# Experts that gather their rows and add weighted results to x1 by accumulating DMAs, in place of a slot scatter

## The reference

```
x1 = layernorm(x + attention(x))                    # (2, 2048, 256)
logits = layernorm(x1, rn_g, rn_b) @ router_w.T + router_b
top_w, top_idx = top_k(logits, 2);  top_w = softmax(top_w)
out = 0
for e in range(8):
    h = layernorm(x1, ln_g[e], ln_b[e])             # same mean and variance, own scale and shift
    h = gelu(h @ w1[e] + b1[e]);  h = h @ w2[e] + b2[e]
    out += combine[..., e] * h                      # combine is top_w where e was chosen, else 0
result = layernorm(x1 + out)
```

## Time and profile before

| what | value |
|---|---|
| median of 3 runs | 3681.25 us (3676.75 to 3688.88) |
| the profiled execution's own time | 3678.63 us |
| its span in the profile | 3677.0 us |
| busy in the span: PE / VectorE / ACT / POOL | 3195.2 / 2888.1 / 2443.3 / 291.8 us |
| mean granted clock of PE | 0.926 of full |

### The profile page before, as it was taken

The page is one execution under the profiler, slowest core; times in us unless marked ns, Lnnn a source line. Parts: engine busy times, 40 slices in busy tenths (PEclk is TensorE's granted clock), DMA queues, the critical chain, the costliest instruction groups (busy, mean ns, idle before and its releaser), DMA issues. The chain is left out here.

```text
span 3677.0 us, 85882 instructions
## 1 busy us (share of the span) xinstructions
PE 3195.2 (87%) x29585; PEld 1513.9 (41%) x29586; DVE 2888.1 (79%) x3223; ACT 2443.3 (66%) x4499; POOL 291.8 (8%) x506
## 2 busy tenths in 40 slices
PE   7849999999999999999999999999844549999970
PEld 3413333333333333333333333333334448999960
DVE  2269999999999999999999999999957503334335
ACT  3309998998999999999899999899801001111110
POOL 0020000000000000000000000000023260000016
PEclk9959999999999999999999999999966659999985
DMA  4520101101011010110110101101064531111114
GB/s 114 125 45 21 28 8 39 28 8 29 21 28 26 24 25 20 30 28 8 39 28 8 29 21 28 26 24 25 16 243 156 202 125 35 37 36 37 36 57 148
DMA packets 127607, 184.40 MB, mean 50 GB/s; under 512 B 23272, under 2 KB 97560, under 8 KB 124412
## 3 DMA queue, kind: packets, MB, share of 16 engines
q1 hardware_dynamic: 119388, 151.03, 15.7%
q0 software_dynamic: 7296, 26.22, 2.1%
q10 hardware_dynamic: 544, 2.10, 0.2%
HBM read 105.36 MB, written 73.93 MB: 49 GB/s over the span
## 5 line engine op out<-in xcount | busy, mean ns | idle before, releaser
L558 DVE TENSOR_REDUCE half_max<-scores 128x2 f32<-128x1024 f32 x2096 | 2387.3, 1212 | 78.8 <-PE scores L461 75.2
L532 ACT ACTIVATE probs<-bank 128x512 f32<-128x512 f32 x4104 | 2227.1, 595 | 211.3 <-PE bank L480 144.4
L512 PE MATMUL bank<-probs,V 128*32 128x256 f32 x16384 | 1319.0, 394 | 68.9 <-ACT probs L532 39.2
L461 PE MATMUL scores<-K,Q 48*128 48x512 f16 x4192 | 832.6, 394 | 50.7 <-DVE half_max L558 24.7
L480 PE MATMUL bank<-Q,K 50*128 50x512 f16 x4104 | 796.0, 381 | 0.3 <-ACT probs L532 0.3
L461 PEld LDWEIGHTS scores<-K,Q 48*128 48x128 f16 x4192 | 201.4, 93 | 940.9 <-DVE half_max L558 739.6
L512 PEld LDWEIGHTS bank<-probs,V 128*32 128x32 f32 x16384 | 323.3, 108 | 628.5 <-issue 545.8
L480 PEld LDWEIGHTS bank<-Q,K 50*128 50x128 f16 x4104 | 375.9, 94 | 117.0 <-ACT probs L532 5.8
L1260 ACT ACTIVATE h<-u 128x1024 f32<-128x1024 f32 x71 | 75.0, 1057 | 420.6 <-DVE u L1287 420.6
L1229 PE MATMUL pre<-xgT,w 128*128 128x128 f32 x2272 | 267.4, 276 | 3.2 <-ACT xgT L1256 2.6
L1229 PEld LDWEIGHTS pre<-xgT,w 128*128 128x128 f32 x2272 | 266.8, 193 | 7.3 <-DVE w L1279 3.8
(11 more groups left out here) (151 smaller groups left out, 1143.0 us busy)
## 6 DMA issues: line engine op xcount, KB each, us to landing
heads<-attended SPq DMA_DIRECT2D x5, 4096.0 KB, 12.9
attended<-att SPq DMA_DIRECT2D x64, 256.0 KB, 2.5
W<-in_L_ffn_w_dram SPq DMA_DIRECT2D x14, 1024.0 KB, 11.6
Q<-q_parts SPq DMA_DIRECT2D x96, 128.0 KB, 5.2
K<-k_parts SPq DMA_DIRECT2D x96, 128.0 KB, 5.6
slot_rows<-zeros POOLq DMA_DIRECT2D x8, 1152.0 KB, 5.2
xg<-slot_rows SPq DMA_DIRECT2D x71, 128.0 KB, 2.0
slot_results<-y SPq DMA_DIRECT2D x71, 128.0 KB, 1.7
```

Of the source, the lines that this page charges most:

```text
L461: mm = nc.tensor.matmul(scores[:, b, h, :], Q[p][r, c, up, t * P:(t + 1) * P], K[p][r, up, kc * TC:(kc + 1) * TC], start=True, stop=True)
L512: mm = nc.tensor.matmul(banks[att_bank[s // KB]][32 * u:32 * u + 32, q], V[wp][:, wk, u // 2, :], probs[:, 4 * s % RING + u, q], start=(wk ...
L532: nc.scalar.activation(probs[:, i % RING, :], banks[tile_bank[i]][:], ACT.Exp, scale=SCALE).then_inc(exp_done, 1)
L558: nc.vector.tensor_reduce(half_max[lc % 2][:, :, up, t, kc], scores[:, b], AX.X, ALU.max).then_inc(max_done[b], 1)
```

## The change

Nothing is scattered into slots, and no result is stored by slot. The route stage turns its table round: for every slot of a tile it works out which token it holds. For each column t of 128 tokens and each choice r VectorE writes a one-hot row of the slot's place in its tile (`row_hot`, 128 columns) and one of its tile times the token's code (`tile_hot`, 72 columns), and a matmul of the two adds the code to the right cell of `coded`; 64 matmuls give the whole table. From it come, in `routes`, three indices for each slot: the row of `xh` to read, the row of `x1` to add to (an empty slot gets one of 128 spare rows behind the 4096), and the place of its weight in `combd`, a new table of token times expert in DRAM.

POOL then gathers the 128 rows of a tile and its 128 weights just before the tile is computed. `ln_g` and `ln_b` are no longer folded into `W1`: ACT applies them, in two instructions with pointers, as it copies the transposed rows. ACT also multiplies `y` by the weights (`ys`), and POOL adds `ys` to `x1` in DRAM with an indirect DMA that accumulates. A token appears in two tiles, so each of these DMAs waits until the one before has landed (`added`). The finish stage then only normalises `x1`. Its row order in DRAM is changed so that a partition's rows lie together. The zeros of `xgd` are no longer written; all 8 `w1` matrices and `b2s` are loaded in the route stage.

```diff
-    xgd = nc.dram_tensor("slot_rows", (NTL * TS, D), F32, kind="Internal").ap()
-    ygd = nc.dram_tensor("slot_results", (USED * TS, D), F32, kind="Internal").ap()
+    x1d = nc.dram_tensor("x1", (T + P, D), F32, kind="Internal").ap()
+    combd = nc.dram_tensor("expert_shares", (T * E, 1), F32, kind="Internal").ap()
...
-        stage_scatter(nc, locals())
...
+            for r in range(2):
+                chain.add(nc.vector.tensor_tensor(part_of[r][:], hot[r][:], over_e(share[r][:]), ALU.mult))
+            chain.wait()
+            nc.vector.tensor_tensor(comb[:], part_of[0][:], part_of[1][:], ALU.add).then_inc(comb_ready, 1)
...
+            for r in range(2):
+                for t in range(NT):
+                    nc.vector.tensor_scalar(row_hot[:, r, t, :], lane[:], place_f[0][:, r, t:t + 1], None, ALU.is_equal
+                                            ).then_inc(hot_ready, 1)
+                    nc.vector.tensor_scalar(tile_hot[:, r, t, :], lane[:, 0:NTL], place_f[1][:, r, t:t + 1],
+                                            token[:, t:t + 1], ALU.is_equal, ALU.mult).then_inc(hot_ready, 1)
+            step(nc.vector.tensor_scalar(owner[:], owner[:], float(E - 1), None, ALU.min))
+            dve.wait_ge(coded_ready, 1)
...
+            def gather(n, q):
+                nc.gpsimd.tensor_copy(cur[q][:], routes[:, bass.ds(n, 1), :].rearrange("p o f -> p (o f)")
+                                      ).then_inc(cur_ready, 1)
+                pool.wait_ge(cur_ready, n + 1)
+                pool.sem_inc(gate, 1)
+                nc.gpsimd.indirect_dma_start(xg[q][:], None, xhd,
+                                             bass.IndirectOffsetOnAxis(ap=cur[q][:, 0:1], axis=0)
+                                             ).then_inc(xg_loaded[q], 16)
+                nc.gpsimd.indirect_dma_start(part[q][:], None, combd,
+                                             bass.IndirectOffsetOnAxis(ap=cur[q][:, 2:3], axis=0)
+                                             ).then_inc(part_loaded[q], 16)
...
+            def step(n, it, q, left):
+                if not isinstance(n, int) or n > 0:
+                    pool.wait_ge(added, 16 * n)
+                if left >= FAR:
+                    if not isinstance(n, int) or n > 0:
+                        pool.wait_ge(turned, n)
+                    pool.wait_ge(ys_ready, n + 2)
+                    pool.sem_inc(gate, 1)
+                    gather(n + FAR, (q + FAR) % GB)
+                pool.wait_ge(ys_ready, n + 3)
+                pool.sem_inc(gate, 1)
+                nc.gpsimd.indirect_dma_start(x1d, bass.IndirectOffsetOnAxis(ap=cur[q][:, 1:2], axis=0),
+                                             ys[q % 2][:], None, compute_op=ALU.add).then_inc(added, 16)
...
-            def copy_rows(n, p):
+            def norm_rows(n, p):
+                e = owner(act, n)
                 act.wait_ge(turned, n + 1)
-                nc.scalar.copy(xgT[p][:], pxT[:, 0:D]).then_inc(xgT_ready, 1)
+                for k in range(KD):
+                    nc.scalar.activation(xgT[p][:, k * P:(k + 1) * P], pxT[:, k * P:(k + 1) * P], ACT.Identity,
+                                         scale=ln_cols[:, 0, bass.ds(e, 1), k], bias=ln_cols[:, 1, bass.ds(e, 1), k]
+                                         ).then_inc(xgT_ready, 1)
...
+            def weigh(n, it, q):
+                act.wait_ge(part_loaded[q], 16 * (it + 1))
+                act.wait_ge(y_ready, n + 3)
+                if not isinstance(n, int) or n > 1:
+                    act.wait_ge(added, 16 * (n - 1))
+                nc.scalar.activation(ys[q % 2][:], y[q % 2][:], ACT.Copy, scale=part[q][:, 0:1]).then_inc(ys_ready, 1)
...
+            for n in range(NC):
+                sp.dma_start(z[:, n], x1d[0:T].rearrange("(p n j) d -> n p j d", p=P, n=NC)[n]).then_inc(z_loaded[n], 16)
...
+            for n in range(NC):
+                moments(n)
+                if n > 0:
+                    normalise(n - 1)
+            normalise(NC - 1)
```

More of the change, by code:

```diff
@@ L304, in stage_attend @@
         att_stored = [sem(f"att_stored{i}") for i in range(2)]
[L305 to L309, removed]
+        gate_pool, gate_dve = sem("gate_pool"), sem("gate_dve")
         ROWS = [(h, i) for i in range(len(Q_PARTS)) for h in range(2)]
@@ L446, in _ @@
                     cut_maxima(it * RC + lc + 2)
[L447 to L450, removed]
         @block.tensor
@@ L1062, in _ @@
             for r in range(2):
-                step(nc.vector.tensor_tensor(took[r][:], hot[r][:], place[:], ALU.mult))
-                step(nc.vector.tensor_reduce(slot_f[r][:], took[r][:], AX.X, ALU.add))
-                nc.vector.tensor_copy(slot[r][:], slot_f[r][:]).then_inc(slots_ready, 1)
-def stage_scatter(nc, a):
-    xhd, xgd, slot, D, E, KD, NCH = (a[n] for n in ("xhd", "xgd", "slot", "D", "E", "KD", "NCH"))
-    EARLY = a["EARLY"]
-    w1, b2, W1, b1c, b2s, ln_cols, IC = (a[n] for n in ("w1", "b2", "W1", "b1c", "b2s", "ln_cols", "IC"))
+                chain.add(nc.vector.tensor_tensor(took[r][:], hot[r][:], place[:], ALU.mult))
@@ new lines, in _, with stage_experts @@
+            step(nc.vector.tensor_tensor(offset[:], above[:], below[:], ALU.add))
+            step(nc.vector.tensor_tensor(goal[0][:], code[:], offset[:], ALU.add))
+            chain.add(nc.vector.tensor_tensor(goal[1][:], goal[0][:], empty[:], ALU.add))
+            step(nc.vector.scalar_tensor_tensor(goal[2][:], goal[0][:], float(E), owner[:], ALU.mult, ALU.add))
+            for i in range(3):
+                nc.vector.tensor_copy(routes[:, :, i], goal[i][:])
+def stage_experts(nc, a):
+    xhd, x1d, combd, W1, W2, b1c, b2s, owner_i, routes, ln_cols = (
+        a[n] for n in ("xhd", "x1d", "combd", "W1", "W2", "b1c", "b2s", "owner_i", "routes", "ln_cols"))
+    KD, IC, D, E, I, USED, ident = (a[n] for n in ("KD", "IC", "D", "E", "I", "USED", "ident"))
+    GB = 4
+    FAR = GB - 1
@@ L1207, in _ @@
-            for n in range(2):
-                load(n, n)
-            for n in range(2):
-                sp.wait_ge(turned, n + 1)
-                load(n + 2, n)
-            run(sp, step)
-            for p in range(2):
-                sp.wait_ge(y_stored[p], 16 * ((USED + 1 - p) // 2) + 1)
+            for s in (y_ready, ys_ready):
+                sp.sem_inc(s, 2)
+            sp.wait_ge(added, 16 * USED)
+        @block.gpsimd
+        def _(pool):
+            def gather(n, q):
[22 more added lines that the diff above has]
+                                             ys[q % 2][:], None, compute_op=ALU.add).then_inc(added, 16)
+            for n in range(FAR):
+                gather(n, n)
+            run(pool, step)
```

368 lines of the change are left out of this document (144 added, 224 removed).

## The result

The changed kernel takes **3622.5 us**, median of 4 runs (3614.7 to 3626.0), against 3679.7 for the kernel before: a ratio of 0.985 [0.983, 0.986]. The forecast was 3532, with 3508 to 3612 as its range. So 57 us were gained where 149 were forecast, and the time lies 10 us above the range.

What follows compares the result with a forecast made beforehand. PE bounds the experts, GpSimd's issuing the scatter and finish: 3677.0 - 106.5 + 22.5 + 1.8 + 10.5 + 2.5 - 79.5 = 3528.3, plus 1.6 and 2.6 gives 3532.5 us; eight in ten, 3508 to 3612.

Steps and rivals of the forecast that it cites:

- Experts, each tile: Expert tiles: GpSimd's serial loop takes 7.4 us a cycle, 0.15 over PE's 7.25, times 70 = +10.5 us.
- the term that I feared most: Accumulating scatter's landing in GpSimd's loop: 1.65 us as plain, plus 0.7 for adding in DRAM, between 0 and 1.89.
- Scatter issue 0.98: GpSimd's loop in each expert tile: issuing the accumulating scatter takes 0.98 us.
- 0.2 for VectorE beside it: Expert tiles: VectorE's copy of `w1` lengthens GpSimd's scatter issue by 0.1 to 0.2 us; 0.2 charged per cycle.
- (1): Expert tiles: GpSimd's loop clearly bounds, an added row costing near the upper end; cycle 8.3, 3595 us, chance 0.18.
- (2): Expert tiles: VectorE's `w1` copy holds up GpSimd's issuing for the whole 1.23 us; cycle 8.4, 3605 us, chance 0.09.
- (3): Expert tiles: ScalarE makes PE wait 0.3 us per tile through dynamic operands and the owner's register load; 3543 us, chance 0.08.
- (4): Expert tiles: slower than before, rows of an accumulating scatter added one after another; cycle 18.3, 4295 us, chance 0.04.
- -106.5: Slot scatter stage goes: 64 scatters (81 us), the wait for the first `xh` load and the last W1 fold; -106.5 us.
- one-hot pairs: Route stage, VectorE: 64 pairs of `row_hot` (0.13) and `tile_hot` (0.15), 17.9 us, part of the route's +22.5 us.
- Start and end: Experts stage: start +1.8 us (5.1 in place of 3.3), end +2.5 us (5.1 in place of 2.6).
- Finish: Finish stage: eight 512 KB loads with moments and normalising, 36.4 us in place of 115.9, -79.5 us; bounds 33 and 46.

Runs made afterwards that it cites:

- experiment 1: Changed kernel with the addition left out of the scatter to `x1` (plain store, sums not the reference's): 3546.2 us.
- experiment 5: Changed kernel in which VectorE copies only one column of each `w1` matrix after the first two tiles: 3574.8 us.
- experiment 3: Changed kernel with eight gather buffers and the gathers for tile n+3 issued before the wait for the last accumulating DMA: 3538.6 us, 0.962 of before.
- experiment 8: Changed kernel with the zeros of `xgd` written again: 3619.7 us; also retraced unedited, the kernel before (3676.3 and 3677.8) and the changed one (3615.9).
- experiment 4: Changed kernel with eight gather buffers instead of four, GpSimd's queue order left as it is: 3609.0 us.
- experiment 7: Kernel that gathers before the wait (3538.6 us), with GpSimd writing the 32 `tile_hot` rows of the second choice: 3538.2 us.
- experiment 2: Changed kernel with VectorE's copy of `w1` written as a multiplication by 1.0: 3617.9 us.

## Why the prediction was wrong

The direction and the places were right; the forecast gain was 92 us too large (149 for 57). To compare the stages I take the third trace of before (span 3676.1) and the second of the changed kernel (3614.0), which entered the route stage within 1.4 us of each other. They are 62.1 apart where the forecast had 148.7:

```profile
2917.71 0.42 DVE L1019 TENSOR_REDUCE best<-lg 128x32 f32<-128x256 f32 x1
L1279 DVE COPY w<-W x71: 1216/1227/1228, 3036.1 to 3540.7; 128x2048 f32 x71
L1298 DVE TENSOR_TENSOR y<-py,b2s x71: 423/425/426, 3054.5 to 3557.6; 128x256 f32<-128x256 f32 x71
L1360 POOL MEMSET f_minus_half<- x1: 101/101/101, 3560.2 to 3560.2; 128x4 f32 x1
```

```profile
2919.11 0.42 DVE L1050 TENSOR_REDUCE best<-lg 128x32 f32<-128x256 f32 x1
L1290 DVE COPY w<-W x71: 1220/1227/1440, 2965.0 to 3551.9; 128x2048 f32 x71
L1310 DVE TENSOR_TENSOR y<-py,b2s x71: 423/425/426, 2987.9 to 3569.9; 128x256 f32<-128x256 f32 x71
L1349 POOL MEMSET f_minus_half<- x1: 102/102/102, 3581.5 to 3581.5; 128x4 f32 x1
```

| piece | before | after | measured | forecast |
|---|---|---|---|---|
| up to the route's first maximum | 2917.7 | 2919.1 | +1.4 | 0 |
| from there to the first copy of `w1` | 118.4 | 45.9 | -72.5 | -84.0 |
| to the first `y` (start) | 18.4 | 22.9 | +4.5 | +1.8 |
| 70 tiles | 503.1 | 582.0 | +78.9 | +10.5 |
| last `y` to the finish | 2.6 | 11.6 | +9.0 | +2.5 |
| finish | 115.9 | 32.5 | -83.4 | -79.5 |

**Experts, each tile: the step that failed**, 68 of the 87 us. The structure was right, all in series on POOL's queue. So was the term that I feared most: landing and the wait behind it came to 2.5 us where 1.65 + 0.7 + 0.3 = 2.65 stood. Two other terms were mis-sized. "Scatter issue 0.98" was taken from a plain scatter; with the addition it is 1.63 (experiment 1), +0.65. I had put the whole price of adding on the DMA engines and none on the engine that issues. "0.2 for VectorE beside it" is 0.68 (experiment 5), +0.48. 7.4 + 0.65 + 0.48 - 0.15 = 8.4, for 8.31 to 8.34 measured. PE's pace, 7.19 on average, was the floor, and the forecast cycle stood just above it; so nothing of this was absorbed and every bit counted 70 times.

**The 0.2** came from a row that I read for its length and not for where it ended. In the earlier trace rows the issue of 1.06 us ended at 2936.61. The first of the two multiplications beside it ended at about 2936.49 (an estimate: they take 0.75 us each, one behind the other from 2935.74), 0.12 before, just as beside the copies of `w1`. Alone the issue would have ended at 2936.51, so little was added; how much depends on where the two meet. The longest of the 64 took 1.27 in the same trace, and 1.44 in the third, where VectorE had begun just before. The "DVE blocks DMA" trap that the prediction weighed (the Trainium skill, page SBUF — State Buffer, section on the two sides of SBUF) says that GpSimd is locked out and cannot write descriptors until the copy ends. The trace agrees: no gather that began less than 0.5 us before a copy, or during it, ended before the copy did. What this costs depends on how much of the copy is still to come: 0.4 to 1.0 us for one issue, 0.68 per tile over the loop. The rule held, and by my reading of one row I had set it aside.

**The rivals.** (1) gave a cycle of 8.3 and that is what came, but from the issuing and not from the landing, which that rival blamed; its number was right by luck. (2) had the mechanism right. Its 1.23 was the upper end of the cost, and I had the accumulating DMA's issue fall on the copy, where it is one of the gathers that does. (3) did not come: ScalarE's two pieces took 0.79 where 0.5 was forecast, which the 0.51 to spare still covered, and in experiment 3 PE never waited. (4) did not come: 128 rows land in 2.5. No rival let two terms be wrong at once, and the range ended just above (2) alone; the two terms that were wrong together lie outside it.

**Route and scatter, +11.5.** -106.5 was true of one execution; the other two spent 7.4 us less there (experiment 8). I had read that the fold ended that stage, and not asked how often it does. The one-hot pairs took 0.37 us each and not 0.28 (the first pair, and the instruction behind the last one, in the first trace of the changed kernel):

```profile
2942.05 0.26 DVE L1111 TENSOR_SCALAR row_hot<-lane,place_f 128x128 f16<-128x128 f16 x1
2942.22 0.30 DVE L1113 TENSOR_SCALAR tile_hot<-lane,place_f,token 128x72 f16<-128x72 f16 x1
2965.74 0.23 DVE L1115 TENSOR_SCALAR owner<-owner 128x72 f32<-128x72 f32 x1
```

That is 23.7 for 17.9, within the bounds of 10 to 31; the route grew by 26.9 for 22.5. PE's matmuls were hidden and W1's loads covered, as said.

**Start and end.** In the table's trace the first product began 7.2 us after POOL's first index copy, where 5.1 were forecast. Of the 2.1 us more, 1.4 are one issue, the first gather's: it ran beside two copies of `w1` in a row (2965.01 to 2967.37), took 2.34 us in place of 0.98 and ended 0.14 us behind them. The clock hardly counts in this pair: PE's first two products took 5.6 and 3.8 us, and 5.3 and 3.8 before. In the first trace of the changed kernel they took 6.4 and 6.7, and the start was 3.6 us longer. There the granted clock was 0.50 all through the route stage, in which PE was busy for 17.9 of 47.7 us, rose after the first product had begun, and stood at 0.64 on average in the second window above: both products ran in part or wholly at the lower level, 1.2 GHz, and PE had stood still for 3.1 us between them. At the end:

```profile
3580.09 0.42 DVE L1310 TENSOR_TENSOR y<-py,b2s 128x256 f32<-128x256 f32 x1 [3.03 <-PE py L1241]
3582.98 1.56 POOL L1206 DMA_INDIRECT x<-ys,cur  x1 [2.98 <-DMA x<-ys,cur]
3591.72 0.10 POOL L1349 MEMSET f_minus_half<- 128x4 f32 x1 [7.18 <-POOLq L1137]
```

The last DMA waited for the one before (2.98), which I had not counted. With 2.5 of the 7.18 for its landing, some 4.7 stay unexplained. The same gap was 5.0 us in experiments 3, 4 and 7, which have eight buffers, and 9.3 in experiment 1, where the landing is shorter; so the landing does not set it, and its cause is open.

**Finish: right** (32.5 for 36.4), with VectorE's chunks 3.11 us apart where 3.36 was forecast.

## What to carry to other kernels

Write down the loop of each issuing engine as a series, and price each issue by its own kind and not by a relative. Where two engines meet, read when the lengthened instruction ends against the end of the other, and not only how long it took: one row with a small cost can hold the whole rule. When such a loop stands close to the pace of the bound engine, take what does not depend on the last DMA ahead of the wait for it, with buffers enough to do so: that turned 3622 us into 3539.

## What the runs showed of the hardware

An indirect DMA of 128 rows of 1 KB that adds in DRAM costs its GpSimd 1.63 us to issue, against 1.00 for one that stores; half the rows cost 1.46. The wait from the end of the issue is 2.5 us against 1.7, and 2.0 with half the bytes.

Around a VectorE copy of 2048 columns (1.23 us) an issue of GpSimd is held until the copy has ended, unless it began more than 0.6 us before. Gathers that began less than 0.5 us before the copy, up to its very start, ended 0.11 to 0.13 us behind it. Those that began later in it ended 0.81 to 0.88 us behind it, which is their own time of 0.95 to 1.01 less 0.13. Both hold for all 52 of them from 3020 to 3480 us, and experiment 2 shows the same beside a multiplication by a constant. Beside two copies (2.36 us) an issue took 2.33. An accumulating issue that began 1.1 us into the copy took its own 1.64 (experiment 3).

GpSimd writes 72 fp16 columns by a two-step comparison in 0.62 us, measured while VectorE wrote its own rows for most of the time, where VectorE needs 0.21 (experiment 7).
